# Forty small list products of an expert, moved from behind the first layer of the expert two ahead of it into that layer's last product

## The reference, cut to what matters

```
logits = flat @ Wr.T
weights, ids = jax.lax.top_k(logits, K)             # K = 2 of E = 8 experts
weights = jax.nn.softmax(weights, axis=-1)
router_weights = zeros((N, E)).at[rows, ids].add(weights)
h = jnp.einsum('nc,efc->nef', flat, W1)              # first layer, 2 F = 512 rows for each expert
val, gate = (h[..., :F], h[..., F:])
act = val * jax.nn.silu(gate)
expert_outputs = jnp.einsum('nef,ecf->nec', act, W2) # second layer
out = jnp.einsum('nec,ne->nc', expert_outputs, router_weights)
```

## Time and profile before

| | |
|---|---|
| median of 3 runs | 1661.7 us (1661.55 to 1662.3) |
| the profiled execution, own time | 1660.71 us |
| its span in the trace | 1659.0 us |
| TensorE busy | 1508.4 us, 91% |
| VectorE busy | 816.6 us, 49% |
| ScalarE busy | 513.9 us, 31% |
| mean granted TensorE clock | 0.956 |

### The profile page before, as it was taken

One profiled execution on the slowest core, in us unless ns is written; L12 is line 12 of the kernel. 1 busy time (PEld: TensorE's weight loads), 2 busy tenths in 40 slices (PEclk: granted clock), 3 DMA queues, 4 the chain that ended last, 5 costly groups with the idle time before them and its releaser, 6 DMA issues.

```text
span 1659.0 us, 21157 instructions
## 1 busy us (share of the span) xinstructions
PE 1508.4 (91%) x8316; PEld 1419.8 (86%) x8316; DVE 816.6 (49%) x1601; ACT 513.9 (31%) x587; POOL 153.3 (9%) x162
## 2 busy tenths in 40 slices
PE   3899999999999999799999899998996559999996
PEld 3889898989898989699999899998995459988885
DVE  6555757565565656612665223452345454544430
ACT  4233333333333342414221233221111224544441
POOL 0112020101010101000000000000000012223321
PEclk7999999999999999899999999999998759999998
DMA  9623131322222225648441043213333656676763
GB/s 290 209 31 52 60 43 60 40 63 37 64 36 66 46 57 127 248 117 220 138 107 47 26 116 94 85 32 83 108 106 108 236 131 180 170 204 173 197 150 73
DMA packets 72745, 183.63 MB, mean 111 GB/s; under 512 B 8987, under 2 KB 39823, under 8 KB 70927
## 3 DMA queue, kind: packets, MB, share of 16 engines
q1 hardware_dynamic: 52550, 135.17, 26.1%
q0 software_dynamic: 20096, 47.10, 15.4%
HBM read 124.15 MB, written 67.93 MB: 116 GB/s over the span
## 4 chain that ended last, share of the span: by engine, by line
PE 79%; ACT 6%; DVE 6%; DMA 4%; issue 3%; SPq 2%; POOL 0%; DVEq 0%; POOLq 0%; ACTq 0%
PE slot L1482 40%; PE slot L1539 11%; PE slot L1715 6%; PE slot L1725 6%; PE kvb L1715 3%; PE slot L1629 3%; PE slot L1620 2%; PE kvb L1597 1%; PE lsb L1583 1%; PE slot L1698 1%; DMA adj_d<-stage 1%; SPq L519 1%; DMA big_lo<-at_d 1%; PE slot L1583 1%; DVE kk_l L1226 1%
## 5 line engine op out<-in xcount | busy, mean ns | idle before, releaser
L1482 PE MATMUL slot<-big_hi,slab_h 128*128 128x418 f32 x1152 | 295.4, 365 | 33.0 <-DMA big_lo<-at_d 9.7
L1482 PE MATMUL slot<-big_lo,slab_h 128*128 128x418 f32 x1152 | 286.4, 357 | 0.0
L1482 PE MATMUL slot<-big_hi,slab_l 128*128 128x418 f32 x1152 | 283.8, 355 | 0.0
L1482 PEld LDWEIGHTS slot<-big_hi,slab_h 128*128 128x128 f32 x1152 | 213.0, 192 | 43.6 <-issue 19.4
L1482 PEld LDWEIGHTS slot<-big_hi,slab_l 128*128 128x128 f32 x1152 | 219.5, 191 | 3.6
L1482 PEld LDWEIGHTS slot<-big_lo,slab_h 128*128 128x128 f32 x1152 | 219.8, 191 | 3.2
L1539 PE MATMUL slot<-adj,xs_h 125*128 125x418 f32 x480 | 118.1, 354 | 0.8 <-DVE ztmp L988 0.5
L703 POOL DMA_DIRECT2D adj_d<-stage x80 | 67.7, 846 | 549.5 <-ACT stage L771 355.0
L1539 PE MATMUL slot<-adj,xs_l 125*128 125x418 f32 x480 | 117.4, 353 | 0.0
L737 POOL DMA_INDIRECT xg<-flat_d,token x32 | 31.2, 974 | 763.4 <-DVE token L1412 646.0
L988 DVE TENSOR_TENSOR slab_l<-slab_raw,slab_h 128x1024 fp32r<-128x1024 f32 x48 | 58.5, 1219 | 82.8 <-ACT slab_h L771 82.7
(11 more groups left out here) (286 smaller groups left out, 2489.7 us busy)
## 6 DMA issues: line engine op xcount, KB each, us to landing
slab_raw<-slabs_dram SPq DMA_DIRECT2D x48, 512.0 KB, 3.7
ws_raw<-w_dram SPq DMA_DIRECT2D x36, 512.0 KB, 5.8
adj_d<-stage POOLq DMA_DIRECT2D x81, 117.2 KB, 3.1
w_raw<-w_dram SPq DMA_DIRECT2D x9, 1024.0 KB, 4.8
adj_d<-eye_dram POOLq DMA_DIRECT2D x1, 6250.0 KB, 25.8
raw<-adj_d SPq DMA_DIRECT2D x3, 1828.8 KB
mix_d<-mixt SPq DMA_DIRECT2D x8, 627.0 KB, 4.0
mix_in<-mix_d SPq DMA_DIRECT2D x8, 627.0 KB, 4.0
```

The source lines that it names most:

```text
L1482: mm = ten.matmul(ps[:, 512 * q:512 * q + CW], w[a][:, kt, :], big[b][:, kt, CW * q:CW * q + CW], start=(kt == 0 and c == 0), stop=(kt == ...
```

## The change

In ROUND, `("LS", e + 2)` goes from behind XE(e+1, 2) and the fourth product to just ahead of VA(e, 1). VectorE follows this new place: its eight list instructions now stand ahead of its two for VA(e, 1). TensorE does not do the list at its place (it skips it for e of 2 and more) but within VA(e, 1): after the three large products of each of kt = 1 to 5 it issues eight of the forty small ones, and the last of them raises the count that the list is full. The lists of experts 0 and 1 stay as they were. GpSimd, ScalarE and the sync engine have no instruction for LS.

```
             m = WS * e + n + 2
             o += [("WP", m)] if m < NWS else []
+            if e + 2 < EXP and n == 3:
+                o.append(("LS", e + 2))
             o.append(key)
...
-        o += [("LS", e + 2)] if e + 2 < EXP else []
         if e + 1 < EXP:
             o.append(("XE", e + 1, NRT - 1))
...
+                def lists_begin(e):
+                    ten.wait_ge(hits_ready, r * EXP + e + 1)
+                    if e:
+                        dved(("LS", e - 1))
+
+                def list_products(e, j):
+
+                    for i in range(NRT):
+                        mm = ten.matmul(lsb[:RT_, 8 * i:8 * i + 6], hit[:, j, RT_ * i:RT_ * i + RT_],
+                                        rec[:, j, e, :], start=(j == 0 and i == 0), stop=(j == NT - 1),
+                                        skip_group_check=True)
+                    return mm
...
                     if kind == "LS":
 
                         e = k[1]
+                        if e >= 2:
+                            continue
...
                         w, xe = ws_p[m % 3], xe_p[k[1] % 2]
+                        lists = k[1] + 2 if kind == "VA" and k[2] == 1 and k[1] + 2 < EXP else None
                         for kt in range(KD):
                             for c, (a, b) in enumerate(COMBOS):
                                 mm = ten.matmul(ps, w[a][:, kt, :], xe[b][:, kt, :],
                                                 start=(kt == 0 and c == 0), stop=(kt == KD - 1 and c == 2))
+                            if lists is not None and 1 <= kt <= 5:
+                                if kt == 1:
+                                    lists_begin(lists)
+                                list_products(lists, 2 * kt - 2)
+                                ls = list_products(lists, 2 * kt - 1)
+                                if kt == 5:
+                                    ls.then_inc(expert_full, 1)
```

More of the change, by code:

```diff
@@ L1685, in _ @@
                         e = k[1]
-                        ten.wait_ge(hits_ready, r * EXP + e + 1)
-                        if e:
-                            dved(("LS", e - 1))
+                        if e >= 2:
+                            continue
+                        lists_begin(e)
                         for j in range(NT):
[L1690 to L1693, removed]
+                            mm = list_products(e, j)
                     elif kind == "XE":
```

## The result

The changed kernel takes 1676.38 us in the median of 6 runs (1674.88 to 1680.31), against 1661.62 before (1659.76 to 1662.98): a ratio of 1.0092, 95% interval 1.0079 to 1.0105. Slower by 14.8 us; the forecast was 15.1 us. The profiled execution took 1677.2 us with a span of 1675.5, 16.5 more than the span before.

A forecast was written before the change was run, and what follows sets the result against it. The chain behind the fourth product, not TensorE's list, was taken to set the stretch to OUT. Added products 14.2 us plus VectorE delay 0.9 gave 15.1 on 1661.7, so 1676.8 us; range 1671 to 1683.

The forecast's parts named there:

- Nothing gained behind the product: Between fourth product and OUT: removing six 1.97 us lists gains 0, as the actt, a_h, a_l, xe_l chain keeps 3.61 us.
- The price within the product: Fourth product on TensorE: five groups of eight small products at 0.47 us each, 14.2 us for six lists.
- The return: Fourth product, taking up large products again behind each group: 0.08 us more, 0.27 in place of 0.19.
- my lower bound: Fourth product: a group's first weights load wholly behind the large product ahead, 0.42 us a group, 12.7 us in all.
- the upper bound: Fourth product: 0.06 us more at each group's beginning, so 0.53 us a group, 16.0 us in all.
- VectorE's list ahead of `actt`: VectorE before actt: the list's eight instructions delay each stretch by 0 to 0.2 us, taken as 0.15, 0.9 in all.
- the signs that I named: Changed profile: fourth product about 7.0 us, idle about 2.1 before OUT, XE to OUT 3.6 to 3.8, actt X + 0.4 to 0.6.
- The gathers: GpSimd's four gathers for expert e+2 begin about 4 us earlier against X: 0, with ±1 us for all.
- The clock: Start of OUT: granted clock falls stay at three of six list stretches, 1.5 us per stretch both ways.
- Rival (a): Start of OUT: the clock falls in all six stretches, three more than now, 4.5 us more, 1681.3 us; chance 11%.
- Rival (b): Fourth product: small products disappear in the large ones and the clock no longer falls, 1658.1 us; chance 2%.
- rival (c): Fourth product: small products alternating with large ones get dearer, near 94 ns, 25 us in all, 1687 us; chance 4%.

## Why the prediction was right

*Nothing gained behind the product.* It rested on expert 6, which had no list and the same X + 3.61. The changed kernel shows the hole in all six, and leaving the products out where they stood brought no time that the runs can tell. This is the step that decides the sign, and the one that the chain of waits would have turned round.

*The price within the product.* 0.47 us a group and 14.2 in all; measured 2.28 us for five, 0.456 a group, 13.7 in all. The return was right: behind a group the first large product is followed after 0.27 or 0.28 us in place of 0.19, 0.08 more. Off were the eight small products, which took 0.37 to 0.38 us and not 8 × 0.049 = 0.39, so that the sum lay between my lower bound and my value. The 0.06 at each group's beginning, from which the upper bound came, isn't there: the first small product starts 0.19 behind the last large one.

*VectorE's list ahead of `actt`.* I took 0.15 us a stretch out of 0 to 0.2, in all 0.9; it is 0.20 in experts 0 and 1 and 0.29 in 2 to 4, in all 1.5. I had the list end 1.44 us behind its start, read to an `xe_l` that followed it; `actt` follows only after 1.64, and the two mistakes, of this term (0.6 us too little) and of the last (0.5 too much), cancelled. That the total came within 0.3 us is therefore luck; that it came within one or two is not. Two of the signs that I named were missed by the same step, if narrowly: `actt` at X + 0.4 to 0.6 (it was X + 0.67 in expert 4) and XE to OUT of 3.6 to 3.8 (3.81 to 3.90, and 4.16 in expert 5). The putting back of VectorE's part shows that the whole of it lies there.

*The gathers.* The first for expert 6 started at 1540.71, X + 1.5 against X + 5.8, so 4.3 us earlier, and no XE of experts 1 to 7 waited for one in either kernel. 0 was right.

*The clock.* I left it at three long OUT in six stretches; they were three of six (0, 1 and 5) and one more behind expert 6. With the last OUT, which fell before and not after, there are four in each profile. That the number was the same is luck as well: the changed kernel's second profile has two falls in the first seven OUT, not four, and 1.5 us hang on each. Rival (a) did not come: two to four of seven, not all. But my reason against it, that expert 6 had kept the clock behind 2.01 us of idle time, was one case and no evidence: with the same stretch and the same idle time expert 6's OUT fell after the change (12.73 us). Rival (b) fell with the group's 0.456 us, rival (c) with the steady spacing within the product.

## What to carry to other kernels

Before moving work off a path, find a place in the same profile where that work is missing and see whether the next step starts earlier; a chain of waits goes through whatever the engine did last and can't say that a wait stood right behind it. Work that fills a hole can be free: the list's 2 us were, to within 3 us for all six. Any other place in a full engine costs the work in whole, and cutting it into groups a little more. Look past the hole, too: forty products put into the empty one cost nothing up to the next step, and a wait of 0.84 us in the step behind it. Shortening the chain (here by doing the transposes one product earlier) made OUT start sooner, 2.0 us in all, and in the profiled execution three falls of the clock went with it, 4.6 us; of the second part one should count on less than one profile shows.

## What the runs showed of the hardware

A fall of the granted clock from 1.00 to 0.50 costs 1.5 us in OUT. Counted by windows of the clock, and not by the length of OUT (in the kernel with the hole filled two OUT are long by a wait), falls at or shortly before OUT came so often:

| time from the last large product to OUT, and what TensorE did in it | falls |
|---|---|
| 2.3 us, 0.9 of them transposes, the rest idle (early XE, no list in the hole or the product; 7 in one profile, one each in two) | 0 of 9 |
| 2.7 us, transposes and the list, never idle (early XE) | 0 of 6 |
| 2.5 to 2.6 us, transposes and idle, small products in the product ahead | 2 of 6 |
| 2.3 us, idle alone (expert 7's OUT, in all twelve profiles) | 8 of 12 |
| 3.6 to 4.2 us, transposes and 1.9 us or more of idle time | 19 of 45 |
| 3.6 to 4.2 us, transposes and 40 small products | 6 of 12 |
| 5.4 us and more, transposes and 80 small products, never idle | 6 of 6 |

The fall of expert 7's OUT in the profile before the change, as a window in it (columns as in the earlier trace rows), and the idle time ahead of that OUT:

```profile
1632.24 0.70 PE L1725 MATMUL slot<-w_h,a_h 128*105 128x512 f32 x2 [2.15 <-DVE a_l L988]
1633.00:1636.40 3.40, 3.40 (x9) 2.35 (x8) 0.00 (x0) 0.00 (x0) 0.00 (x0) 0.50 0.00 0
```

Among the stretches with transposes the falls are on the whole more frequent the longer the stretch is, and at 3.6 to 4.2 us it makes no difference that can be seen whether small products or idle time fill it. In the longest, the clock fell while TensorE had not been idle at all. Length alone does not decide it, as expert 7's OUT shows: 2.3 us of idle time and nothing else, and most fell. That stretch differs in what precedes it too (its four products have no XE between them), so the cause stays open. The Trainium skill ("TensorE: Matmul & The Clock Gate", Part 4, "PE-mode transpose") says that transposes don't count for the clock as products do. No run here has transposes alone in such a stretch; the falls among the 5.4 us of transposes and small products agree with it, and the 0 of 9 beside the 8 of 12 at the same 2.3 us, with and without transposes, don't bear it out. That two of six fell behind only 2.5 to 2.6 us, where the product ahead held the list, is one profile's showing; whether the small products in it are the cause stays open.
